# Mixer order: decays in two halves a slot, turned outputs and step sizes behind the probabilities, choice of experts and its scatters ahead of the scan

## The reference

```python
x = x + xattn(layernorm(x), ctx)     # 16 heads; q = qdq(x) @ qdq(wq).T, softmax over 1601 keys, qdq on the output
x = x + mamba(layernorm(x))          # xp = x @ x_proj.T ; dt = softplus(low @ dt_proj.T + b)
                                     # h = exp(dt*A)*h + dt*x*B over 64 tokens, 16 states ; y = sum_n C*h + D*x
x = x + moe(layernorm(x))            # softmax over 64 experts, top 8, each expert keeps the first 512 tokens in token order
```

## Time and profile before

| | us |
|---|---|
| median of 3 runs | 2489.81 (2484.97 to 2494.7) |
| the profiled execution | 2486.63 |
| its span, first to last instruction | 2484.9 |
| mean granted TensorE clock | 0.944 of full speed |

### The profile page before, as it was taken

How to read it: one execution, slowest core, us unless ns; L and a number is a source line. 1 busy time by engine, 2 the same in 40 slices (tenths; PEclk the granted TensorE clock), 3 DMA queues, 4 the chain that set the end, 5 groups by cost and what they waited for, 6 DMA issues and landing times. The chain is left out here.

```text
span 2484.9 us, 55791 instructions
## 1 busy us (share of the span) xinstructions
PE 2136.3 (86%) x21320; PEld 1461.4 (59%) x21320; DVE 1786.6 (72%) x3776; ACT 1432.3 (58%) x2948; POOL 674.2 (27%) x708
## 2 busy tenths in 40 slices
PE   5999999999999999999999999999995089899940
PEld 3666666566666666666666666666663067666730
DVE  4557777878777778787777878787777655555538
ACT  1667666767676667676666667676765144444410
POOL 1002030312222130303030303121220447766650
PEclk9999999999999999999999999999996589999975
DMA  6486662313132323132232333231310156555647
GB/s 202 165 285 231 201 237 76 82 66 83 68 84 76 73 80 85 66 92 89 60 97 52 97 84 79 70 82 67 84 53 34 43 178 187 174 177 181 185 144 270
DMA packets 132950, 294.14 MB, mean 118 GB/s; under 512 B 22139, under 2 KB 89383, under 8 KB 126544
## 3 DMA queue, kind: packets, MB, share of 16 engines
q1 hardware_dynamic: 114256, 255.89, 33.6%
q0 software_dynamic: 18432, 34.69, 3.9%
HBM read 165.40 MB, written 108.27 MB: 110 GB/s over the span
## 5 line engine op out<-in xcount | busy, mean ns | idle before, releaser
L623 PE MATMUL W<-sb_ident,sb_probs 128*128 128x128 f32 (+1 forms) x3328 | 487.6, 282 | 59.8 <-issue 19.5
L783 ACT ACTIVATE sb_probs<-S,sb_negmax 128x1604 f32<-128x1604 f32 x256 | 409.5, 1600 | 224.0 <-DVE sb_negmax L948 221.7
L775 ACT ACTIVATE sb_probsT<-W 128x384 f32<-128x384 f32 (+1 forms) x1024 | 476.1, 514 | 72.1 <-PE W L623 66.9
L623 PEld LDWEIGHTS W<-sb_ident,sb_probs 128*128 128x128 f32 (+1 forms) x3328 | 366.9, 140 | 189.5 <-issue 93.8
L948 DVE TENSOR_REDUCE sb_negmax<-S 128x1 f32<-128x1604 f32 x256 | 465.9, 1820 | 1.5 <-PE S L613 0.3
L596 PE MATMUL W<-sb_wkv_in,sb_ctx 128*128 128x256 f32 (+1 forms) x1664 | 434.0, 405 | 26.7 <-DVE sb_K_lo L932 13.9
L586 PE MATMUL W<-sb_ctx,sb_wkv_in 128*32 128x401 f32 x4096 | 410.6, 503 | 2.5 <-DVE sb_V L942 2.5
L596 PEld LDWEIGHTS W<-sb_wkv_in,sb_ctx 128*128 128x128 f32 (+1 forms) x1664 | 306.7, 194 | 99.3 <-ACT sb_probsT L775 33.0
L767 ACT ACTIVATE sb_K_hi<-W,sb_pair_cols 128x401 fp32r<-128x401 f32 x256 | 153.0, 598 | 336.8 <-PE W L586 259.0
L932 DVE SCALAR_TENSOR_TENSOR sb_K_lo<-W,sb_pair_cols,sb_K_hi 128x401 fp32r<-128x401 f32 x256 | 161.9, 633 | 223.4 <-ACT sb_K_hi L767 221.5
L1279 POOL DMA_INDIRECT y_scratch<-sb_ys,sb_places x256 | 258.3, 1009 | 112.3 <-issue 91.6
(11 more groups left out here) (181 smaller groups left out, 2819.7 us busy)
## 6 DMA issues: line engine op xcount, KB each, us to landing
sb_ctx<-ctxT SPq DMA_DIRECT2D x32, 1604.0 KB, 7.7
xe_scratch<-sb_none SPq DMA_DIRECT2D x32, 1088.0 KB, 12.5
sb_xg<-xe_scratch SPq DMA_DIRECT2D x64, 544.0 KB
sb_BC<-bc_scratch SPq DMA_DIRECT2D x32, 1024.0 KB, 6.3
sb_Q_hi<-sb_q_hi SPq DMA_DIRECT2D x128, 128.0 KB, 4.4
sb_Q_lo<-sb_q_lo SPq DMA_DIRECT2D x128, 128.0 KB, 5.8
y_scratch<-sb_none SPq DMA_DIRECT2D x16, 1024.0 KB
sb_rows<-y_scratch SPq DMA_DIRECT2D x16, 1024.0 KB, 7.5
```

The lines of the kernel that those rows point to most:

```text
L623: ins = pe.transpose(W[0:keys_in(t), at * P:(at + 1) * P], probs[n % 2][:, t * P:t * P + keys_in(t)], ident[:])
L775: act.activation(probsT[k][n % (k + 1)][:, 0:wide], ring[bank_of("T", G, k)][:, 0:wide], ACT.Copy)\
L783: act.activation(probs[n % 2][:].rearrange("p (c k) -> p c k", c=QUADS), scores_of, ACT.Exp, bias=negmax[:, slot:slot + 1], accum_out=den[ ...
```

## The change

It alters the order of work in the mixer; the arithmetic is the same.

1. ACT: the four decays of a unit are made in two pairs. The first pair stands ahead of `soft`, the second ahead of `k_up`; before, all four stood behind `k_up`. The exponential of the softplus goes behind the third copy of probabilities, its logarithm behind `k_up`.
2. PE: O0, O1 and O3 go from place 0 to place 1, O2 too; `dt` goes from place 0 to place 1 of slot 7. On DVE `norm_o` goes behind `v_up`, and the whole softplus goes behind `v_up` too, its last three steps behind `k_low`.
3. DVE: `route_begin` (five of the eight searches) goes to slot 5, the other three (`route_found`) and `route_end` to slot 6; before, it was slot 6 and slot 8.
4. POOL: the scatter of the pair two turns back goes ahead of the scan's inputs; in turn 16, the last with a scan, it goes behind all of them.

```diff
--- before.py
+++ after.py
@@ -52,9 +52,9 @@
 LAG = 4
 END = SLOTS * (PAIRS + 1) + LAG
 
-MIX = {(4, 0): ["O3"], (5, 0): ["oqT"], (5, 1): ["proj"], (6, 0): ["ln2T"], (6, 1): ["xp"], (7, 0): ["dt"],
-       (8, 0): ["XQ"], (8, 1): ["Q"], (10, 0): ["O0"], (14, 0): ["O1"], (1, 0): ["yT"],
-       (2, 0): ["O2", "ln3T"], (2, 1): ["logits"], (3, 2): ["pos"]}
+MIX = {(4, 1): ["O3"], (5, 0): ["oqT"], (5, 1): ["proj"], (6, 0): ["ln2T"], (6, 1): ["xp"], (7, 1): ["dt"],
+       (8, 0): ["XQ"], (8, 1): ["Q"], (10, 1): ["O0"], (14, 1): ["O1"], (1, 0): ["yT"],
+       (2, 0): ["ln3T"], (2, 1): ["O2", "logits"], (3, 2): ["pos"]}
 
 QS = NS // 4
 UNITS = 2 * NS // QS
@@ -524,16 +524,18 @@
                 if prev:
                     pool.wait_ge(dve_up, dve_at(i - 1, "V2"))
                     pool.tensor_tensor(st[:, 9:10], st[:, 8:9], neg_half[:], ALU.pow).then_inc(pool_up, 1)
+                if ended and i != PAIRS:
+                    scatter(i - 2)
                 if prev:
                     for unit in range(UNITS // 2):
                         scan_input(i - 1, unit)
                 if nxt:
                     part_q(i + 1)
-                if ended:
-                    scatter(i - 2)
                 if prev:
                     for unit in range(UNITS // 2, UNITS):
                         scan_input(i - 1, unit)
+                if i == PAIRS:
+                    scatter(i - 2)
             pool.wait_ge(scattered, 16 * TOPK * PAIRS)
 
 
@@ -791,13 +793,15 @@
                     act.wait_ge(ring_full, full_at("O", n // STRIPS - 2))
                 act.activation(OT[n // STRIPS % 2][32 * s:32 * s + 32, :], O[32 * s:32 * s + 32, 0:P], ACT.Copy).then_inc(ot_up, 1)
 
-            def decay(p, unit):
+            def decay(p, unit, part):
 
                 h, q = divmod(unit, NS // QS)
-                act.wait_ge(dve_up, dve_at(p, "U" if h == 0 else "S" + UNIT_NAMES[unit - 4]))
-                for n in range(QS):
+                if part == 0:
+                    act.wait_ge(dve_up, dve_at(p, "U" if h == 0 else "S" + UNIT_NAMES[unit - 4]))
+                for n in range(part * QS // 2, (part + 1) * QS // 2):
                     ins = act.activation(abar[q][:, n, :], dt_[:, h, :], ACT.Exp, scale=A[:, h, q * QS + n:q * QS + n + 1])
-                ins.then_inc(act_up, 1)
+                if part == 1:
+                    ins.then_inc(act_up, 1)
 
             for n in range(STRIPS):
                 k_up(n)
@@ -812,24 +816,27 @@
                     turned(G, 1)
                 if strip and G % SLOTS in NO_VALUES:
                     turned(G, 2)
+                scanned = p is not None and 0 <= m - FIRST_DECAY < UNITS
+                if scanned:
+                    decay(p, m - FIRST_DECAY, 0)
                 if G < ALL_STRIPS:
                     soft(G)
-                if m == 3 and p is not None:
-
-                    act.wait_ge(dve_up, dve_at(p, "Z"))
-                    act.activation(ez, negz, ACT.Exp).then_inc(act_up, 1)
                 if strip and G % SLOTS not in NO_VALUES:
                     turned(G, 2)
                 if m == 3 and p is not None:
 
+                    act.wait_ge(dve_up, dve_at(p, "Z"))
+                    act.activation(ez, negz, ACT.Exp).then_inc(act_up, 1)
+                if strip:
+                    turned(G, 3)
+                if scanned:
+                    decay(p, m - FIRST_DECAY, 1)
+                if G + STRIPS < ALL_STRIPS:
+                    k_up(G + STRIPS)
+                if m == 3 and p is not None:
+
                     act.wait_ge(dve_up, dve_at(p, "EZ"))
                     act.activation(lz, ez1, ACT.Ln).then_inc(act_up, 1)
-                if strip:
-                    turned(G, 3)
-                if G + STRIPS < ALL_STRIPS:
-                    k_up(G + STRIPS)
-                if p is not None and 0 <= m - FIRST_DECAY < UNITS:
-                    decay(p, m - FIRST_DECAY)
                 if m == 14 and p is not None:
 
                     act.wait_ge(dve_up, dve_at(p, "LOGITS"))
@@ -1004,14 +1011,6 @@
                     link(dve.tensor_tensor(x_res[:], x_res[:], bp_row[:], ALU.add))
                 if m == 2:
                     copy_out("ln2T", p, ln2T[:].rearrange("p k t -> p (k t)"))
-                if m == 3:
-                    W = bank("dt", p)
-                    dve.wait_ge(ring_full, full_at("dt", p))
-                    link(dve.tensor_scalar(z[:, 0, :], W[:, 0:P], cols[:, DTB, 0:1], None, ALU.add))
-                    dve.tensor_scalar(z[:, 1, :], W[:, P:2 * P], cols[:, DTB, 1:2], None, ALU.add).then_inc(ring_free["dve"], 1)
-
-                    dve.wait_ge(ring_free["dve"], free_at("dt", p))
-                    up(dve.scalar_tensor_tensor(negz, z[:], -1.0, z[:], ALU.mult, ALU.min))
                 if m == 13:
 
                     after(dve, x3_out, 16 * p)
@@ -1060,15 +1059,18 @@
                     link(dve.tensor_copy(dlT[:], W[:, 0:P]))
                     dve.tensor_copy(BCT[:], W[0:2 * NS, P:2 * P]).then_inc(ring_free["dve"], 1)
                 if m == 3:
+                    W = bank("dt", p)
+                    dve.wait_ge(ring_full, full_at("dt", p))
+                    link(dve.tensor_scalar(z[:, 0, :], W[:, 0:P], cols[:, DTB, 0:1], None, ALU.add))
+                    dve.tensor_scalar(z[:, 1, :], W[:, P:2 * P], cols[:, DTB, 1:2], None, ALU.add).then_inc(ring_free["dve"], 1)
+
+                    dve.wait_ge(ring_free["dve"], free_at("dt", p))
+                    up(dve.scalar_tensor_tensor(negz, z[:], -1.0, z[:], ALU.mult, ALU.min))
 
                     dve.wait_ge(act_up, act_at(p, "EXPZ"))
                     up(dve.tensor_scalar(ez1, ez, 1.0, None, ALU.add))
                     dve.wait_ge(dve_up, dve_at(p, "EZ"))
                     link(dve.scalar_tensor_tensor(negz, ez1, 1.0, ez, ALU.subtract, ALU.subtract))
-                    dve.wait_ge(act_up, act_at(p, "LNZ"))
-                    link(dve.tensor_tensor(negz, lz, negz, ALU.subtract))
-                    link(dve.scalar_tensor_tensor(dt_[:], z[:], 0.0, negz, ALU.max, ALU.add))
-                    up(dve.tensor_tensor(u[:], dt_[:], ln2T[:], ALU.mult))
                 if m == 13:
                     dve.wait_ge(pool_up, pool_at(p, "R3"))
                     after(dve, scattered, 16 * TOPK * p)
@@ -1079,6 +1081,11 @@
                     dve.tensor_copy(pr2[:], bank("logits", p)[:, 0:E]).then_inc(ring_free["dve"], 1)
             def rest_c(p, m, link):
 
+                if m == 3:
+                    dve.wait_ge(act_up, act_at(p, "LNZ"))
+                    link(dve.tensor_tensor(negz, lz, negz, ALU.subtract))
+                    link(dve.scalar_tensor_tensor(dt_[:], z[:], 0.0, negz, ALU.max, ALU.add))
+                    up(dve.tensor_tensor(u[:], dt_[:], ln2T[:], ALU.mult))
                 if m == 15:
                     W = bank("pos", p)
                     dve.wait_ge(ring_full, full_at("pos", p))
@@ -1091,13 +1098,19 @@
                 return dve.scalar_tensor_tensor(junk[:, t, :], iota_e[:], idx[:, t:t + 1], slotv[:], ALU.is_equal,
                                                 ALU.mult, accum_out=slot_[:, t:t + 1])
 
+            FIND = TOPK // 2 + 1
+
             def route_begin(p):
                 link = Chain(dve, dve_r, p, ROUTE_LINKS)
                 link(dve.tensor_copy(idx, topi[:]))
-                for t in range(TOPK):
+                for t in range(FIND):
+                    find_slot(t)
+                return link
+
+            def route_found(link):
+                for t in range(FIND, TOPK):
                     ins = find_slot(t)
                 link(ins)
-                return link
 
             def route_end(p, link):
                 link(dve.scalar_tensor_tensor(pos, idx, -float(CAP), slot_, ALU.mult, ALU.add))
@@ -1131,17 +1144,19 @@
                     strip_max(G)
                 if m == 0:
                     link = Chain(dve, dve_b, p, B_LINKS, pause[:]) if mix else None
-                for job in small_at(G, 0):
-                    if job[0] == "O":
-                        norm_o(job[1])
                 if slot == 8 and nxt:
                     x_up(i + 1)
                 if mix and m < 15:
                     rest_a(p, m, link)
                 if v:
                     v_up(*v)
-                if slot == 8 and i >= 2:
-                    route_end(i - 2, route_link)
+                for job in small_at(G, 1):
+                    if job[0] == "O":
+                        norm_o(job[1])
+                if slot == 5 and i >= 2:
+                    route_link = route_begin(i - 2)
+                if slot == 6 and i >= 2:
+                    route_found(route_link)
                 if mix and m == 15:
                     rest_a(p, m, link)
                 if mix:
@@ -1149,7 +1164,7 @@
                     if 0 <= m - FIRST_DECAY - 1 < UNITS:
                         scan_unit(p, m - FIRST_DECAY - 1, link)
                 if slot == 6 and i >= 2:
```

(15 more changed lines are left out.)

## The result

| | before | after |
|---|---|---|
| median, us | 2487.39 (2484.93 to 2494.70, 4 runs) | 2517.06 (2516.10 to 2517.75, 4 runs) |
| span of the profiled execution | 2484.9 | 2515.4 |
| mean granted TensorE clock | 0.944 | 0.939 |

The ratio is 1.011, with a 95% interval of 1.0087 to 1.0132: the change costs 29.7 us. That is inside the range given (2440 to 2524), but the time went up by 1.1% where 0.3% less was forecast.

The account below looks back on a forecast made before the run. PE, busy 94% in the mixer, was taken as the bound, with a standstill behind the scatter. Plus 10, minus 11, minus 7 made minus 8: median 2481 us, 2458 to 2501; 8 in 10, 2440 to 2524.

Parts of the forecast that it names:

- Scatter and routing, slots 10 and 11: Slots 10 and 11 together fall to about 13.9 us once the scatter leaves: minus 6.6 a turn.
- The scatter at its new place: Scatter early in slot 7 holds PE again, into slot 8: plus 7.3 a turn, net plus 0.7, plus 10 in all.
- the slower rival: PE's hold behind the scatter also takes in slot 7's keys, adding 2.8: plus 39, 2520 us; chance 0.22.
- a chain of maximum, exponential, copy and query product: Serial work in slot 8 after PE is let go, before slot 9 begins: 5.4 to 6.6 us.
- a half clock in slot 9: Up to 1.6 us more a turn if the halved PE clock behind the scatter reaches into slot 9.
- The rival that the hold needs the scan beside it: PE stops only when scatter and DVE scan run together, so the move ends it: 2393 us; chance 0.15.
- O steps behind T3: Waits go in slots 10, 14 (0.2 each) and 2 (0.3), nothing in 4; with dt, minus 0.8 a turn, minus 11.
- dt behind T3: Slot 7: 0.5 less wait, but 0.1 waiting for the copy of values.
- Softplus later: Its last step comes 1.3 to 2 later, directly ahead of slot 8's maximum; PE's standstill behind the scatter covers it.
- The price without cover: The later softplus would cost 1 to 1.4 a turn if PE were not held behind the scatter.
- Decays in halves: First half hides in ACT's wait for the maximum; second delays high keys by up to 0.25: nothing.
- The last turns: Turn 16: 8.85 of scan delay and 1.2 of routing go, four times 0.7 come back: minus 7.

Follow-up runs that it names:

- e1_scatter: Kernel before with only the routing in slots 5 and 6 and the scatter ahead of the scan's inputs: 2505.65 us, ratio 1.0067.
- e2_places: Kernel before with only the O steps, dt, `norm_o` and softplus moved, including the softplus's two ACT steps: 2519.31 us, ratio 1.0122.
- e3_halves: Kernel before with only ACT's decays made in two pairs: 2468.65 us, ratio 0.9925.
- a_same: The changed kernel, unaltered, run on the third chip against the kernel before there: 2428.72 us, ratio 1.0011.
- b_same: The kernel before, unaltered, profiled on the third chip: 2426.47 us, one run.

## Why the prediction was wrong, point by point

*Scatter and routing, slots 10 and 11: right.* They were to fall to 13.9 and fell to 7.39 and 6.82, 14.2 together.

*The scatter at its new place: right in place, and in size with some luck.* First DMA 1.37 into slot 7 (1 to 2 foreseen), release 11.6 behind it (11.8), half clock behind the release, slot 8 plus 7.68 (7.3, from 5.6 to 8.7), net plus 0.75 a turn (0.7). The parts of that size were not the ones I had added up. The keys of slot 7 were held, as the slower rival said, but not at its price of 2.8 more. From release to slot 9 I had counted a chain of maximum, exponential, copy and query product, 5.4 to 6.6, and it took 8.0: PE's own work behind the low keys, without a pause and mostly at half clock. Of the steps that the rival put in series only the keys stand ahead of that work; softplus and maximum ran beside it. The 1.6 at most for a half clock in slot 9 (its basis says 5.6 where the sum has 5.4) did not come true: 1.00 from 1167. The near hit of 7.68 against 7.3 is thus in part luck. Alone, in e1_scatter, the move cost 1.4 a turn in slots 8 to 11, 17 us in all, against plus 10 and minus 7 counted.

*The rival that the hold needs the scan beside it fell:* in slot 7 and 8 no scan runs, and PE was held as long. That one would have given 2393. It rested on a reading that was too early: PE's stop of 0.92 in the earlier trace rows begins at 1161.13, behind the seventh DMA (1160.29), not the sixth.

*"O steps behind T3" and "dt behind T3", together minus 0.8 a turn, minus 11: this step failed.* In the changed kernel slots 2, 4 and 7 lost 0.99 a turn, about 14 us in fourteen turns. Slots 14 and 15 took 13.00 together, where they take 12.18 with the decays in halves and the O step at its old place: 0.82 more a turn. With the softplus, e2_places measured plus 31. I priced whom the moved job waits for and who waits for DVE, but not what the list does to the job behind it. A job may start when the one three places ahead is copied out. With an O step at place 0 the order (`ln3T` left out) is T1, O, V, T2, T3, logits, and the logits wait for V, copied early by DVE. With it at place 1 the order is T1, V, T2, T3, O, logits, and the logits wait for T2, whose copy stands behind the exponential on ACT. In slot 2 of the changed kernel ACT is in that exponential until 1113.00, and PE stands (timelines of ACT and of PE):

```profile
1111.42 1.60 ACT L785 ACTIVATE sb_probs<-S,sb_negmax 128x1604 f32<-128x1604 f32 x1 [1.71 <-DVE sb_negmax L955]
...
1113.00 0.97 ACT L777 ACTIVATE sb_probsT<-W 128x512 f32<-128x512 f32 x2
```

```profile
1112.37 0.33 PE L653 MATMUL W<-sb_ident,sb_OT 128*128 128x128 f32 x1
1113.64 0.66 PE L698 MATMUL W<-sb_gateT,sb_oqT 128*128 128x64 f32 x4 [0.95 <-ACT sb_probsT L777]
```

So slot 2 lost 0.58 where I counted 0.3 gained. In slots 4 and 7 the keys inherit T2's bank in the same way (0.3 at most each), and O3 and `dt` wait for the copy of values besides, 0.7 and 0.3 at most. Slot 14 gained 0.49, more than the 0.2 counted, but less than the 0.88 that the decays give it alone. PE's rows show why nothing is left of their gain in slot 15: V waits there for the low keys, which it does not in e3_halves (timeline of the changed kernel, turn 9):

```profile
1210.52 1.08 PE L598 MATMUL W<-sb_wkv_in,sb_ctx 128*68 128x256 f32 x4 [0.36 <-DVE sb_K_lo L939]
```

How the O step delays the low keys was not taken apart.

*Softplus later, "the hold covers it": right.* In the changed kernel the query product waits for ACT's copy once between 200 and 1860 us (1.1, the row for L576 above), in e2_places and a_same fourteen times (15.7 each). And slot 9 begins 8.0 behind the release, sooner than the 8.51 of e1_scatter, where the softplus is at its old place. The price without cover, 1 to 1.4, was right too: slot 8 lost 1.19 in e2_places, where the hold stands in slot 10, and in a_same, where there is none.

*Decays in halves, priced at nothing: wrong for the edit alone, minus 20.* I had put what they free under the O steps' gain in slot 14. It is theirs alone: slot 14 gained 0.88 and slot 15 0.40 with no O step moved. In the changed kernel most of this is lost again: slots 14 and 15 are 7.10 and 5.90, just as in e2_places, which has no halves.

*The last turns, minus 7: right for the scans, nothing of it in the total.* The scans end 7.1 earlier against the last scores, and the experts' first product 4.6. The rest of the span grew from 490.8 to 496.0 and gave that back. Why is open; on the third chip the same stretch is 487.4 and 488.9, and 2.5 are left of the gain.

*What stays open.* Why TensorE is held behind the scatter on one chip and not on two others; whether the moved rows or the working out of the transfers do it; whether pairs of DMAs take it away there; and what the O steps, `dt` and the softplus cost each by itself. None of the runs with pairs or with rows out of bounds ran on that chip.

## What to carry to other kernels

In a ring of banks a moved job changes the predecessor of every job around it: write the list out before and after, and price the wait of the job behind the moved one first. A gain booked under one part of a change may belong to another, so time each part alone, and compare stage by stage with the whole: here a sum that agreed hid that one part took 0.82 of another's gain of 1.28 a turn. On two chips a run of eight indirect DMAs on POOL was better dealt out in pairs among POOL's other work (ratio 0.985, and on one of them 0.993 in fours), since what it delays collides later with the scans on DVE.

## What the hardware showed that was not expected

- One program, three chips: 2488 us on one, 2424.6 and 2424.8 on the others. Most of the difference lies in the mixer: its last scores begin at 1885.1 on the first chip and at 1829.2 on the third. Slots 10 and 11 take 20.7 on the first and 13.9 on the third, from the hold behind the scatter. Slot 12 gives part of it back, 6.48 against 8.48.
- So the same edit costs 1.1% on the one chip and 0.1% on another (1.011 against 1.0011).
- On the third chip a scan beside two scan inputs of POOL takes 3.04 for 1.23, and an indirect DMA beside a scan 1.70 for 0.97. The clock falls to 0.62 behind V's wait of 1.80 in turn 9 (windows of b_same), and likewise in turns 5 and 13. Slot 12 takes 10.1 in these three and 8.5 in the others:

```profile
1139.00:1143.00 4.00, 3.53 (x10) 2.80 (x11) 2.31 (x3) 1.82 (x3) 1.21 (x1) 0.62 0.99 345
```
